# Expert layer of a two-layer transformer: the capacity threshold by bits with counts on TensorE, up products before down products, the last norm in two halves

## The reference

```python
h = layernorm(x) * (1 + scale) + shift                    # 1024 x 256
logits = h @ gate_w + expert_bias                         # 7 routed experts
aff = sigmoid(logits)
mask = best 2 of 7 experts of each token
score = where(mask, aff, -1.0).T                          # 7 x 1024
_, sel_idx = top_k(score, capacity)                       # capacity = 1024 // 7 = 146
# each expert keeps its 146 best tokens; ties go to the earlier token
ffn(h, w1, w2): x1, x2 = split(h @ w1); (x1 * silu(x2)) @ w2
out = x + gate * (shared_ffn(h) + sum over routed experts of weight * ffn_e(h))
```

## Time and profile before

| | |
|---|---|
| time, median of 3 runs | 858.86 us (857.44 to 860.13) |
| the profiled execution: time, span | 859.08 us, 857.3 us |
| mean granted TensorE clock | 0.934 of full speed |
| TensorE busy | 727.9 us (85% of the span) |
| VectorE busy | 615.7 us (72%) |
| ScalarE, POOL busy | 478.8 us (56%), 376.4 us (44%) |

### The profile page before, as it was taken

The page is one execution under the profiler, slowest core; times in us unless marked ns, Lnnn a source line. Parts: engine busy times, 40 slices in busy tenths (PEclk is TensorE's granted clock), DMA queues, the critical chain, the costliest instruction groups (busy, mean ns, idle before and its releaser), DMA issues. The chain is left out here.

```text
span 857.3 us, 13269 instructions
## 1 busy us (share of the span) xinstructions
PE 727.9 (85%) x4368; PEld 630.3 (74%) x4368; DVE 615.7 (72%) x1313; ACT 478.8 (56%) x961; POOL 376.4 (44%) x389
## 2 busy tenths in 40 slices
PE   4769999899998999999999589972889998579980
PEld 2558888788887888878888489972667786548870
DVE  3645776667666776766776798986488878569988
ACT  2445666656675666755665434324587867155761
POOL 1193565515655156550451250002445544037883
PEclk9778999999999999999999989985899999889995
DMA  7340000000000000000000000004000000000001
GB/s 269 108 120 7 13 26 13 14 1 14 25 15 13 0 13 12 13 13 1 7 7 7 1 1 2 1 1 148 1 1 0 1 1 1 1 1 2 1 0 50
DMA packets 19723, 19.77 MB, mean 23 GB/s; under 512 B 1998, under 2 KB 17870, under 8 KB 19662
## 3 DMA queue, kind: packets, MB, share of 16 engines
q1 hardware_dynamic: 18334, 17.84, 6.6%
q10 hardware_dynamic: 1328, 1.18, 0.5%
HBM read 17.97 MB, written 1.05 MB: 22 GB/s over the span
## 5 line engine op out<-in xcount | busy, mean ns | idle before, releaser
L1000 POOL TENSOR_TENSOR at_swapped<-at_swapped,at_sin 128x512 f32<-128x512 f32 x40 | 51.7, 1292 | 180.0 <-ACT at_swapped L781 180.0
L816 ACT ACTIVATE at_probs<-at_probs,at_negmax 128x128 f32<-128x128 f32 (+7 forms) x128 | 99.5, 778 | 27.7 <-DVE at_negmax L895 24.5
L895 DVE CUSTOM_DVE_ANT_0 at_probs<-at_scores,causal 128x128 f32<-128x128 f32 (+7 forms) x128 | 96.4, 753 | 24.1 <-PE at_scores L698 21.9
L709 PE MATMUL at_turn<-ident_sb,at_probs 128*128 128x128 f32 x576 | 86.7, 278 | 12.2 <-DVE at_full_T_lo L910 11.4
L709 PEld LDWEIGHTS at_turn<-ident_sb,at_probs 128*128 128x128 f32 x576 | 67.6, 142 | 20.6 <-issue 6.5
L808 ACT ACTIVATE at_edge_T_hi<-at_turn 128x128 fp32r<-128x128 f32 (+3 forms) x128 | 55.5, 434 | 41.4 <-PE at_turn L709 41.1
L696 PE MATMUL at_scores<-at_kT_hi,room 128*128 128x512 f32 (+1 forms) x192 | 69.2, 360 | 10.6 <-POOL room L1022 5.1
L697 PE MATMUL at_scores<-at_kT_lo,room 128*128 128x512 f32 (+1 forms) x192 | 68.5, 357 | 0.0
L698 PE MATMUL at_scores<-at_kT_hi,room 128*128 128x512 f32 (+1 forms) x192 | 68.2, 355 | 0.0
L808 ACT ACTIVATE at_full_T_hi<-at_turn 128x512 fp32r<-128x512 f32 x64 | 38.3, 599 | 50.1 <-PE at_turn L709 48.3
L910 DVE TENSOR_TENSOR at_edge_T_lo<-at_turn,at_edge_T_hi 128x128 fp32r<-128x128 f32 (+3 forms) x128 | 61.3, 479 | 2.4 <-ACT at_edge_T_hi L808 2.4
(11 more groups left out here) (360 smaller groups left out, 2467.3 us busy)
## 6 DMA issues: line engine op xcount, KB each, us to landing
at_wq_in<-L_attn_Wqkv SPq DMA_DIRECT2D x16, 128.0 KB, 2.2
at_wo_in<-L_attn_Wo SPq DMA_DIRECT2D x16, 128.0 KB, 2.1
staging<-L_ffn_routed_w SPq DMA_DIRECT2D x7, 256.0 KB, 4.2
wmod<-L_wmod SPq DMA_DIRECT2D x3, 512.0 KB, 8.1
wmod<-L_wmod SPq DMA_DIRECT2D x1, 1536.0 KB, 11.4
x<-L_attn_x ACTq DMA_DIRECT2D x1, 1024.0 KB, 6.2
at_wkv_in<-L_attn_Wqkv SPq DMA_DIRECT2D x8, 128.0 KB, 4.7
staging<-L_ffn_w_gate SPq DMA_DIRECT2D x1, 1024.0 KB, 5.3
```

Source lines behind the costliest of these rows:

```text
L709: mm = pe.transpose(p_turn[t % 2][:, b - b0, :], probs[:, s % 4, b * P:(b + 1) * P], m.ident[:, :])
L816: act.activation(row, row, ACT.Exp, scale=-1.0, bias=negmax[:, s % 4:s % 4 + 1], accum_out=rowsum[:, s // NT % 2, i:i + 1])\
L895: dve.tensor_tensor_reduce(out=probs[:, s % 4, 0:width], in0=p_scores[s % 2][:, 0:width], in1=m.causal[:, S - width:], scale=-1.0, scalar= ...
L1000: pool.tensor_tensor(swapped[:, b, :], swapped[:, b, :], sin[:, cols], ALU.mult).then_inc(rope_turned, 1)
```

## The change

Four things are done in one edit.

1. The last norm is no block of its own. Its first four tiles (`FIRST_TILES`) are normed, transposed and split at the end of `attention1`, between the last residual adds; the other four at the beginning of `ffn1`. The normalisation goes from VectorE to ScalarE, with the negative mean times rstd (`spread`) as its bias. One chain semaphore and one pair of square-root semaphores serve all stages; elsewhere this renames only.
2. The threshold of each expert is built from the top bits of its float value downwards, three bits a round, ten rounds. In each, VectorE sets eight bounds per expert (`compare`), compares all scores of 128 partitions with them, TensorE counts over the partitions with a matrix of ones in 8 small products (`count`), and VectorE keeps the largest bound that at least 146 scores reach (`raise_cut`). Ties are ordered by 16 small products (`find_order`) and `weigh` makes the weights. Score, cut and counts lie in PSUM.
3. All 16 up products come first, in `slots`, from slot 4 on with a count behind each; then all 8 down products. `mid` is made on VectorE straight from PSUM, `fed` is kept for all experts, and the copies to `y` and of x1 are gone.
4. The routed results are added straight from PSUM as each expert's down product ends: tiles 2 to 7 on VectorE (42 operations as before), tiles 0 and 1 by ScalarE and POOL.

The core of the diff (signatures and renamed semaphores left out):

```diff
+def spread(dve, m, tiles):
+    cols = slice(tiles[0], tiles[-1] + 1)
+    return dve.scalar_tensor_tensor(out=m.nbias[:, cols], in0=m.meanvar[:, cols, 0], scalar=-1.0, in1=m.rstd[:, cols], op0=ALU.mult, op1=ALU.mult)
...
-    transposed_rows(nc, m, sems, sb, 1, 6, "ln3")
...
@@ attention1, TensorE, at the end @@
+                pe.wait_ge(ln_normed, len(FIRST_TILES))
+                for k in range(KD):
+                    for n in FIRST_TILES:
+                        mm = pe.transpose(ln_banks[k][:, n * P:(n + 1) * P], ln_xn[:, n, k * P:(k + 1) * P], m.ident[:, :])
+                    mm.then_inc(ln_turned, 1)
@@ attention1, ScalarE, at the end @@
+                load_table(act, m, ACT.Sqrt, 0)
+                variance_roots(act, m, FIRST_TILES, 5)
+                act.wait_ge(spread_ready, 1)
+                for n in FIRST_TILES:
+                    act.activation(ln_xn[:, n, :], m.x[:, n, :], ACT.Identity, scale=m.rstd[:, n:n + 1], bias=m.nbias[:, n:n + 1]).then_inc(ln_normed, 1)
+                for k in range(KD):
+                    act.wait_ge(ln_turned, k + 1)
+                    act.activation(ln_h32[:, k, :], ln_banks[k], ACT.Identity, scale=m.modcol[:, 1, 8 + k:9 + k], bias=m.modcol[:, 1, 6 + k:7 + k])\
+                        .then_inc(ln_scaled, 1)
+                variance_roots(act, m, LAST_TILES, 6)
@@ attention1, VectorE, at the end @@
+                add_out(1, 0)
+                add_out(1, 1)
+                final_stats(FIRST_TILES)
+                add_out(1, 2)
+                variances(dve, m, chain, FIRST_TILES)
+                add_out(1, 3)
+                inverse_roots(dve, m, chain, FIRST_TILES, 5)
+                spread(dve, m, FIRST_TILES).then_inc(spread_ready, 1)
+                final_stats(LAST_TILES)
+                variances(dve, m, chain, LAST_TILES)
+                for k in range(KD):
+                    cols = slice(0, BANK)
+                    dve.wait_ge(ln_scaled, k + 1)
+                    chain.run(dve.tensor_copy(m.hT.hi[:, k, cols], ln_h32[:, k, :]))
+                    dve.tensor_tensor(m.hT.lo[:, k, cols], ln_h32[:, k, :], as_f32(m.hT.hi[:, k, cols]), ALU.subtract)
@@ ffn1 @@
+        by_row, p_aff, p_marked, score, p_kept = (part(2, n * NT * E8) for n in range(5))
+        cut = p_y[2][:, 1, DM - E8:DM]
+        counts, order = part(3, 0), part(3, DM)
+        POOL_TILES, OWN_TILES = (0, 1), (2, 3, 4, 5, 6, 7)
+        slots = [(0, 0), (1, 0), (0, 1), (1, 1)] + [(e, c) for e in range(2, E8) for c in range(2)]
+        GATED_SLOTS = (0, 1, 2)
@@ ffn1, TensorE @@
+                def count(r):
+                    pe.wait_ge(compared, r + 1)
+                    out = counts[:, :, :].rearrange("p t e -> p (t e)")
+                    for t in range(NT):
+                        mm = pe.matmul(out, ones[:, :], above[:, t, :, :].rearrange("p j e -> p (j e)"), start=(t == 0), stop=(t == NT - 1))
+                    mm.then_inc(counted, 1)
+                def find_order():
+                    pe.wait_ge(split_done, 2)
+                    pe.matmul(order[:, :, :], earlier[:, :], equal[:, :, :], start=True, stop=False)
+                    for t in range(NT):
+                        pe.matmul(order[:, :, :], ones[:, :], more[:, t:t + 1, :].broadcast_to([P, NT, E8]), start=False, stop=False)
+                    for t in range(NT - 1):
+                        rest = NT - 1 - t
+                        mm = pe.matmul(order[:, t + 1:, :], ones[:, :], equal[:, t:t + 1, :].broadcast_to([P, rest, E8]), start=False, stop=(t == NT - 2))
+                    mm.then_inc(ordered, 1)
...
+                find_logits(0)
+                up(0)
+                turn_x()
+                up(1)
+                pe.wait_ge(hT_ready, KD)
+                find_logits(1)
+                up(2)
+                turn_logits()
+                up(3)
+                for n in range(FIRST_ROUND, len(slots)):
+                    up(n)
+                    if n < ORDER_SLOT:
+                        count(n - FIRST_ROUND)
+                    elif n == ORDER_SLOT:
+                        find_order()
+                for e in range(E8):
+                    down(e)
@@ ffn1, VectorE @@
+                def middle(n):
+                    dve.wait_ge(x2_read, n + 1)
+                    if n >= 2:
+                        dve.wait_ge(fed_lo, n - 1)
+                    gate = act2[:, n % 2, :]
+                    if n in GATED_SLOTS:
+                        chain.run(dve.tensor_tensor(gate, p_x2[n % 2][:, :], gate, ALU.mult))
+                    dve.tensor_tensor(mid[:, n % 2, :], p_x1[n % 2][:, :], gate, ALU.mult).then_inc(mid_done, 1)
+                def compare(r):
+                    as_int = mybir.dt.int32
+                    digits = steps[:, r, :].unsqueeze(2).broadcast_to([P, DIGIT, E8])
+                    chain.run(dve.tensor_tensor(bounds[:, :, :].bitcast(as_int), cut.bitcast(as_int).unsqueeze(1).broadcast_to([P, DIGIT, E8]),
+                                                 digits, ALU.bitwise_or))
+                    dve.tensor_tensor(above[:, :, :, :], score[:, :, :].unsqueeze(2).broadcast_to([P, NT, DIGIT, E8]),
+                                      bounds[:, :, :].unsqueeze(1).broadcast_to([P, NT, DIGIT, E8]), ALU.is_ge).then_inc(compared, 1)
+                def raise_cut(r):
+                    dve.wait_ge(counted, r + 1)
+                    chain.run(dve.scalar_tensor_tensor(out=reached[:, :, :], in0=counts[:, :, :], scalar=float(CAPACITY), in1=bounds[:, :, :],
+                                                        op0=ALU.is_ge, op1=ALU.mult))
+                    chain.run(dve.tensor_reduce(cut if r + 1 < ROUNDS else last_cut[:, :], reached[:, :, :].rearrange("p j e -> p e j"), AX.X, ALU.max))
...
+                for n in range(FIRST_ROUND, len(slots)):
+                    r = n - FIRST_ROUND
+                    if r < ROUNDS:
+                        raise_cut(r)
+                        if r + 1 < ROUNDS:
+                            compare(r + 1)
+                        else:
+                            split_ties()
+                    elif n == ORDER_SLOT:
+                        weigh()
+                    middle(n)
...
                     for i, t in enumerate(OWN_TILES):
                         returned(dve, e, t)
...
+                        dve.scalar_tensor_tensor(out=m.x[:, t, :], in0=p_y[t // 2][:, t % 2, :], scalar=row_weight[:, t, e - 1:e], in1=m.x[:, t, :],
                                                  op0=ALU.mult, op1=ALU.add).then_inc(routed_added, 1)
```

More of the change, by code:

```diff
@@ L1780, in ffn1 @@
-        scaled = x1[:, :, 0:DM]
+        mask, row_weight = buf("mask", [P, NT, E8]), buf("row_weight", [P, NT, E8])
+        logits = buf("logits", [NE, S])
+        steps = buf("steps", [P, ROUNDS, DIGIT], mybir.dt.int32)
+        bounds, reached = buf("bounds", [P, DIGIT, E8]), buf("reached", [P, DIGIT, E8])
+        above = buf("above", [P, NT, DIGIT, E8], BF16)
+        more, equal = buf("more", [P, NT, E8], BF16), buf("equal", [P, NT, E8], BF16)
+        kept, last_cut = buf("kept", [P, NT, E8]), buf("last_cut", [P, E8])
@@ L1828, in up, with turn_logits @@
+                def turn_logits():
+                    pe.wait_ge(logits_read, 2)
+                    for t in range(NT):
+                        mm = pe.transpose(by_row[:, t, 0:NE], logits[:, t * P:(t + 1) * P], m.ident[0:NE, 0:NE])
+                    mm.then_inc(logits_turned, 1)
+                def up(n):
+                    e, c = slots[n]
                     pe.wait_ge(w1_ready, e + 1)
-                    n = 2 * e + c
-                    for half, (bank, read) in enumerate(((p_x1, x1_read), (p_x2, x2_read))):
+                    for half, bank in enumerate((p_x1, p_x2)):
@@ L1940, in _ @@
+                load_table(act, m, ACT.Silu, 2)
+                feed_hi(2)
+                for n in range(3, len(slots)):
+                    e, c = slots[n]
+                    activate(n)
+                    if c == 1 and e + 2 < E8:
+                        split_hi(e + 2)
+                    feed_hi(n)
+                for e in range(1, E8):
+                    scale(e)
             @block.vector
             def _(dve):
-                def feed_lo(e):
-                    dve.wait_ge(fed_hi, 2 * e + 2)
-                    out = fed[e % 2][:, BANK:S]
-                    dve.tensor_tensor(out.lo, mid[:, 1, :], as_f32(out.hi), ALU.subtract).then_inc(fed_lo[1], 1)
@@ L1947, in add_shared, with split_lo @@
-                def add_shared():
-                    for j in range(PAIRS):
-                        dve.wait_ge(down_mm, j + 1)
-                        rows = m.x[:, 2 * j:2 * j + 2, :]
-                        dve.tensor_tensor(rows, p_y[j][:, :, :], rows, ALU.add).then_inc(shared_added, 1)
-                chain = Chain(dve, rank_chain)
-                for e in range(2):
+                chain = m.chain.on(dve)
+                def split_lo(e):
```

(10 more changed lines are left out.)

468 lines of the change are left out of this document (213 added, 255 removed).

## The result

829.68 us in the median of four executions (827.95 to 833.65), against 858.35 before: a ratio of 0.967 (0.963 to 0.971), 28.7 us faster. I had said 839.5 and at best 835; the direction was right and the gain half as large again as forecast, outside the stated range of 835 to 847. A second series gave 829.75, ratio 0.966 (0.964 to 0.969). The profiled execution took 828.47 us, span 826.7.

The account below looks back on a forecast made before the run. TensorE was taken as the bound except in the last norm and the updates after the threshold search. Terms -5.2 - 3.1 + 7.0 - 18.1 = -19.4 from 859.08 gave 839.7, stated as 839.5 us; range 835 to 847 for 8 in 10.

Parts of the forecast that it names:

- the price of a count: Search rounds on TensorE: eight small 64-column products taken at 0.75 us, ten rounds 7.5 (6.8 to 9.2; 18.4 at low clock).
- the order: The 16 find_order products on TensorE: 1.3 us (1.3 to 1.9).
- the stall: Around up(4): marking the best two and the first comparison end 0.3 us after it; 0.5 put in the sum.
- the +7.0: Part 3, TensorE from four up products done to the last down product: 65.8 us instead of 58.8.
- the early part: Kernel start to the second attention's second residual add: no instruction added, so change 0.
- the late part: Second attention's second residual add to the kernel's end: all forecast terms lie here, -19.4 us.
- Part 1: Last norm, split between residual adds and normalised on ScalarE: expert stage begins near 749.3 instead of 754.53, -5.2 us.
- Part 2: Front of the expert stage, to the end of four up products: 18.2 us instead of 21.3, -3.1 us.
- Part 4: End after the last down product: updates from PSUM at 0.40 us run beside down products; 4.5 instead of 22.6, -18.1 us.
- (b): Search rounds do not fit, moderately: POOL waits or small products near 1.2 us, ten rounds 0.6 dearer, 845.5; chance 0.13.
- (c): POOL holds all four VectorE operations of a round, 1.04 us each: ten times 3.1 more, 870.5; chance 0.03.
- (d): TensorE's clock falls in the slots: 2.3 us per slot, half of twelve 14, 853.5; chance 0.03.

Follow-up runs that it names:

- counts_wide: Changed kernel with the counts' comparison results and matrix of ones in 4-byte instead of 2-byte numbers; 835.55 us, ratio 0.975.
- old_norm: Changed kernel with the last norm again a block of its own, all eight tiles on VectorE, search and product order still new; 834.72 us, ratio 0.974.
- warm: Changed kernel plus 26 unread products, 16 behind the attention's last output product and 10 behind the norm's eight transposes; 828.52 us, ratio 0.967.
- half_search: Kernel before with the search cut from 18 to 9 full rounds, order on TensorE kept; 856.47 us, ratio 1.0004.
- updates_sbuf: Changed kernel with the 42 updates reading their first operand from the staging buffer in SBUF instead of PSUM; 836.44 us, ratio 0.976.
- half_search_early: Kernel before with 9 search rounds and the weight transposes moved behind the fifth expert's up products; 847.18 us, ratio 0.989.
- norm_shared: Changed kernel with two of the first four norm tiles normalised by VectorE instead of ScalarE; 830.82 us, ratio 0.968.

## Why the prediction missed

The step that failed most is the price of a count. The sum had "Ten rounds 7.5 (6.8 to 9.2 ...)" and 1.3 for the order; both bounds were rows of 4-byte transposes, and the counts are 2-byte numbers. Measured: 3.7 for the ten counts (34.23 us from 761.14 to 795.37, less eleven up products of 2.75 and the stall; 0.34 each once the slots are steady), 0.25 for the stall (forecast 0.5), 795.83 - 795.37 = 0.46 for find_order's 16 products. That is 4.9 us less; the twelve up products took 33.1 instead of 33.6 and the down products 23.2 instead of 22.9, and the +7.0 became +1.9. counts_wide shows that the bounds were good ones for the wrong type (0.91 in a range of 0.68 to 0.92). A lower bound from a row of another operand type is none. No product in the trace of before had the right type, so the lower end should have been left open.

The second step that failed: the early part was put at nothing, on the ground that the renaming and the shared chain "add no instruction". It gave 3 us in the medians (28.7 less the 25.7 by which the late part fell, 120.2 to a mean of 94.5). The kernels with nothing but the added buffer, input and semaphores show 2.5 of them, from a cause that stays open; the rest is within the spread. The profiled pair has 4.7.

Part 1: -6.5 against -5.2. The four normalisations ended 6.9 us after the second add instead of 7.3, the transposes took 1.44 instead of 1.84, and the first product came 0.31 after VectorE's last split instead of 0.7. Part 2: -3.5 against -3.1, right with its reasons (old_norm); the clock rose 3.4 us after the stage's start, the second half waited 0.62 (0.8 said). What its slow start still cost, warm shows: 1.0 to 1.5 us.

Part 4: -17.8 against -18.1 and the updates at 0.40 start to start (six in 2.44), as chosen. What stood behind it was only half right: TensorE's order held the weights at least as long as the search did (half_search), and the price of the updates was decided by where their operand lies (updates_sbuf, half_search_early).

Of the rivals none came. (b) and (c) need idle of TensorE in the slots, or small products near 1.2 us; there is 0.25 us of idle in all ten, and a count costs 0.34. (d) needs a low clock, and it was 1.00 from 749.02 to 821.87. The range failed because it leaned to one side: the ten rounds could be dearer by up to 10.9 us (18.4 for 7.5), but cheaper by only 0.7.

Added up by the measured parts: 6.3 us from the late part (25.7 less 19.4) and 3 from the early one make 9.3 of the 9.8 by which 839.5 missed 829.7; the other 0.5 is the median of before, 858.86 in the forecast and 858.35 in the result.

## What to carry to other kernels

Price a small product by a row with the same operand type: eight products of 64 columns cost 0.34 us here with 2-byte and 0.91 with 4-byte numbers, so ten counts on TensorE cost under 4 us if the flags are 2-byte. When a busy engine seems to hold the end, look also where the instruction that hands its result on stands in the other engine's order; halving 22 us of search gained nothing until that instruction was moved. Compare two kernels from a mark behind which they differ: that distance repeated within about 1 us, while whole times of the kernel before lay between 854.2 and 860.6.

## What the runs showed of the hardware

- Eight 2-byte products of 64 columns, each with its load of 128 weights, cost 0.34 us in the stream, the same with 4-byte numbers 0.91; the loads of one group take 98 and 191 ns. With seven of the eight left out a count is 0.21 us shorter, 0.03 for each.
- A VectorE update with both operands in SBUF went from 0.475 to up to 0.97 us beside POOL's work, and POOL's adds from 0.74 to 0.91 in the mean. With the first operand in PSUM the slowest update took 0.485.
- In the changed kernel TensorE's granted clock was 1.00 while it stood idle for 4.12 us before the transposes, 0.71 in them, and 0.50 (the 1.2 GHz level) in the 2.58 us of idle behind them and in the first 3.37 us of the expert products. In norm_shared, with 3.13 us of idle, the transposes still had 1.00. In warm, where products that nobody reads fill the idle but for 0.39 and 0.62 us, it was 1.00 (the 2.4 GHz level) from 737.03 to 747.17.
- The kernel before with an unused buffer of 32 bytes per partition measured 0.34% less (0.16 to 0.52%), and executions over 857 us were 2 of 8 instead of 17 of 25 on the same chip. The cause is open.
